# Token tiles turned by VectorE, a column-grouped gate, and seven early expert tiles in a top-2 expert layer

## The chip, the cores and the metric

The kernel runs on one core of a Trainium2 chip. The metric is device time in microseconds, the median of the runs shown. The core's engines run their own instruction streams and meet at semaphores: PE (TensorE) multiplies, DVE (VectorE) and ACT (ScalarE) work on its results, POOL (GpSimd) issues the indirect DMAs, and SP (SyncE) issues plain ones. All float32 products of the expert layer are made of three float32r products (high by high, high part by low weight, low part by high weight).

## The reference

```python
W = weights[condition]                       # (64 sequences, 64, 64)
y = jnp.einsum('bct,bcd->bdt', x, W)         # x is (64, 64, 1024): 4096 tokens of 1024
logits = y @ W_gate + b_gate                 # 8 experts
_, top_idx = jax.lax.top_k(logits, 2)
y_all = jax.nn.relu(jnp.einsum('bsd,edh->bseh', y, W_e) + b_e)
out = x + jnp.take_along_axis(y_all, top_idx[..., None], axis=2).mean(axis=2)
```

Each token goes through two of eight 1024x1024 experts, chosen by its own logits.

## The kernel before, in words

**Token tiles.** The 4096 tokens are 32 tiles of 128 rows, in eight groups of G = 4. For each tile `product` multiplies the block-diagonal condition matrices by the tile of x (two matmuls, 512 columns each) into `psO`; ACT copies it to `ys`, with the features of one token put in four quarters, and sends it to `y_rows` in DRAM, from which tokens are later gathered. PE turns `ys` with eight transposes into `psT` (`transposes`), ACT copies it out as the high part (`high`), DVE takes the low part (`low`). When a group is turned, `gate` multiplies it by the gate's weights in 16 matmuls of 512 columns; `unstack` turns the logits back; DVE picks the two experts of each token (`logits`, `choose`, `masks`); `ranks` counts on PE which slot each choice takes in its expert's list; `slots` makes addresses; POOL's `route` writes the token numbers to `slot_table` in DRAM, eight indirect DMAs a group.

**Expert tiles.** A tile is 128 slots of one expert, 48 matmuls of 512 columns (`products`). The first EARLY = 5 belong to expert 0 and are gathered straight from `y_rows` by a few indices (`early`), turned by PE and multiplied before the whole table is known. The rest wait for it: ACT reads all of `slot_table`, DVE makes the indices, POOL gathers each tile with four indirect DMAs (`gather`), DVE turns it with one 32x32-block transpose (`turn_rows`), ACT and DVE make the high and low parts (`parts`), PE multiplies (`all_products`), DVE adds the bias (`finish`), ACT takes the relu and half, and POOL adds the rows to `out` with an accumulating scatter. `schedule` on DVE works out which tile belongs to which expert; its result is needed by the first tile past the early ones.

**What sets the order.** Every stream is written by hand and in order; a wait holds up all that stands behind it on its engine. On SP, `turn` loads the tile of x four ahead when a product is done. `out` must first hold x, because the results are added to it: twelve tiles are stored from SBUF (`store`, slots 2 and 3 of the middle groups), and ten copies of two tiles each go from DRAM to DRAM (`copy`) behind the last load. Expert 0's weights are loaded in eight chunks by POOL and split into high and low parts on ACT and DVE (`split_first`), expert 1's by SP behind the copies. Per group PE runs four products, four sets of transposes, two halves of a gate, an `unstack` and a `ranks`.

## Time and profile before

| what | us |
|---|---|
| median of three runs | 924.06 (922.05 to 924.29) |
| profiled execution, its own time | 923.56 |
| its span in the trace | 921.8 |

The span runs from the first to the last record; 1.8 us of the time lie around it. A timeline row gives start, duration, engine, line and what it writes and reads, with the idle time ahead of it and who ended that. "PEclk" is the clock that TensorE was granted, as a share of 2.4 GHz.

### The profile page before, as it was taken

What the parts mean: (1) busy time and instruction counts of PE and PEld (TensorE: products, weight loads), DVE (VectorE), ACT (ScalarE), POOL (GpSimd) and SP (SyncE); (2) the same over time, 40 slices, a digit from 0 to 9 for tenths busy, and PEclk for the clock granted to TensorE, in tenths of its full rate; (3) what the DMA queues carried; (4) which work ended last, traced back from release to release, by engine and by line L of the source; (5) the groups of instructions that cost most, each with busy time, mean ns of one, the idle gap of its engine ahead of it and who ended that gap; (6) DMA issues with size and microseconds to landing.
All of it is one profiled execution on the core that took longest, in us unless ns stands there. A gap on an engine that the chain in (4) does not pass through costs nothing.

```text
span 921.8 us, 16408 instructions
## 1 busy us (share of the span) xinstructions
PE 892.2 (97%) x3988; PEld 702.6 (76%) x3989; DVE 408.6 (44%) x600; ACT 293.0 (32%) x383; POOL 497.7 (54%) x549
## 2 busy tenths in 40 slices
PE   8899989999999999999999999999999999999992
PEld 5455547788888888888888888888888888888882
DVE  4376776246373337333733354335533543333320
ACT  6586852225152123111521141113321421112210
POOL 4036465457666655655565546753655475555420
PEclk9999998999999999999999999999999999999997
DMA  8999979939686449454864476545854645444433
GB/s 320 402 368 361 374 290 319 304 82 256 158 284 133 102 94 292 95 111 97 260 138 97 91 201 186 110 103 127 254 110 92 193 102 114 91 97 98 81 46 46
DMA packets 51391, 163.11 MB, mean 177 GB/s; under 512 B 14178, under 2 KB 14178, under 8 KB 51202
## 3 DMA queue, kind: packets, MB, share of 16 engines
q0 software_dynamic: 26480, 77.78, 39.1%
q1 hardware_dynamic: 18546, 67.65, 20.5%
q10 hardware_dynamic: 6336, 17.34, 4.8%
q8 instruction: 12, 0.20, 0.1%
q14 instruction: 17, 0.14, 0.0%
HBM read 102.28 MB, written 70.94 MB: 188 GB/s over the span
## 4 chain that ended last, share of the span: by engine, by line
PE 87%; DMA 4%; POOL 3%; issue 3%; DVE 1%; SPq 0%; ACT 0%; ACTq 0%; POOLq 0%; DVEq 0%
PE psO L524 78%; PE psO L460 4%; DMA rows<-in_x 3%; POOL slot_table L344 3%; PE psT L476 2%; PE psG L486 1%; PE psG L488 1%; DMA rows<-y_rows,first 1%; PE psR L499 1%; POOL rows L359 0%; DVE w_lo L793 0%; POOL out L397 0%; SPq L271 0%; DVE rows L910 0%; DVE w_lo L797 0%
## 5 line engine op out<-in xcount | busy, mean ns | idle before, releaser
L524 PE MATMUL psO<-w_hi,a_hi 128*128 (+1 forms) x1104 | 340.6, 390 | 0.3 <-issue 0.3
L524 PE MATMUL psO<-w_lo,a_hi 128*128 (+1 forms) x1104 | 339.9, 389 | 0.0
L524 PE MATMUL psO<-w_hi,a_lo 128*128 (+1 forms) x1104 | 339.9, 389 | 0.0
L371 POOL DMA_INDIRECT rows<-y_rows,idx_g x256 | 263.8, 1030 | 110.6 <-issue 55.3
L524 PEld LDWEIGHTS psO<-w_hi,a_lo 128*128 128x128 f32 x1104 | 207.2, 188 | 43.1
L524 PEld LDWEIGHTS psO<-w_lo,a_hi 128*128 128x128 f32 x1104 | 207.2, 188 | 43.1
L524 PEld LDWEIGHTS psO<-w_hi,a_hi 128*128 128x128 f32 x1104 | 206.6, 188 | 43.5 <-issue 1.1
L935 DVE TENSOR_TENSOR a_lo<-ys,a_hi 128x1024 fp32r<-128x1024 f32 x64 | 78.4, 1226 | 115.3 <-ACT a_hi L693 115.3
L687 ACT ACTIVATE ys<-ys 128x1024 f32<-128x1024 f32 x34 | 36.1, 1061 | 271.3 <-DVE ys L910 271.3
L687 ACT ACTIVATE rows<-rows 128x1024 f32<-128x1024 f32 x35 | 37.1, 1061 | 265.8 <-DVE rows L910 265.8
L344 POOL DMA_INDIRECT slot_table<-toks,idx_all x64 | 64.1, 1002 | 77.1 <-DVEq L847 59.7
L910 DVE TENSOR_TENSOR ys<-psO,bias 128x1024 f32<-128x1024 f32 x34 | 41.6, 1222 | 135.1 <-PE psO L524 119.4
L910 DVE TENSOR_TENSOR rows<-psO,bias 128x1024 f32<-128x1024 f32 x35 | 42.8, 1224 | 129.0 <-PE psO L524 108.5
L924 DVE STREAM_TRANSPOSE ys<-rows 128x1024 f32<-128x1024 f32 x64 | 79.2, 1238 | 5.4 <-DMA rows<-y_rows,idx_g 5.2
L804 DVE TENSOR_TENSOR w_lo<-raw,w_hi 128x1024 f32 x56 | 65.1, 1222 | 34.4 <-ACT w_hi L641 34.4
L397 POOL DMA_INDIRECT out<-rows,idx_s x32 | 59.7, 1865 | 38.2 <-POOL idx_s L393 16.5
L397 POOL DMA_INDIRECT out<-ys,idx_s x32 | 55.5, 1736 | 42.0 <-ACT ys L687 20.7
L367 POOL COPY idx_g<-idx_all 128x4 uint32 x64 | 25.6, 400 | 88.1 <-issue 56.4
L693 ACT CAST a_hi<-ys 128x1024 fp32r<-128x1024 f32 x64 | 66.8, 1044 | 9.3 <-issue 8.9
L460 PE MATMUL psO<-rows,raw 128*128 128x512 f32 x128 | 62.3, 609 | 4.6 <-DMA rows<-in_x 4.0
L793 DVE TENSOR_TENSOR w_lo<-psT,w_hi 128x512 fp32r<-128x512 f32 x64 | 41.4, 686 | 40.4 <-ACT w_hi L627 37.4
L641 ACT CAST w_hi<-raw 128x1024 f32 x56 | 55.1, 1048 | 3.0 <-DMA raw<-in_L_ffn_W_e 2.2
(115 smaller groups left out, 417.0 us busy)
## 6 DMA issues: line engine op xcount, KB each, us to landing
raw<-in_L_ffn_W_e SPq DMA_DIRECT2D x56, 512.0 KB, 6.0
rows<-in_x SPq DMA_DIRECT2D x32, 512.0 KB, 7.2
y_rows<-ys ACTq DMA_DIRECT2D x32, 512.0 KB, 7.3
out<-rows SPq DMA_DIRECT2D x12, 512.0 KB, 6.3
bias<-in_L_ffn_b_e SPq DMA_DIRECT2D x8, 512.0 KB, 7.6
rows<-y_rows,idx_g POOLq DMA_INDIRECT x256
raw<-in_L_ffn_W_e POOLq DMA_DIRECT2D x4, 512.0 KB, 12.2
bias<-in_L_ffn_W_e POOLq DMA_DIRECT2D x4, 512.0 KB, 15.0
```

What stands on the lines that cost most here:

```text
L344: pool.indirect_dma_start(out=table, out_offset=bass.IndirectOffsetOnAxis(ap=adr[:, g, r, s:s + 1], axis=0), in_=toks[:, n:n + 1], in_offs ...
L371: pool.indirect_dma_start(out=rows[:, slot, a * DQ:(a + 1) * DQ], out_offset=None, in_=y_parts, in_offset=bass.IndirectOffsetOnAxis(ap=idx ...
L397: pool.indirect_dma_start(out=out, out_offset=bass.IndirectOffsetOnAxis(ap=idx_s[:, m:m + 1], axis=0), in_=o_sb[m], in_offset=None, comput ...
L460: last = nc.tensor.matmul(psO[s % 2][:, h * BANK:(h + 1) * BANK], bd[:, s, :], rows[:, s, h * BANK:(h + 1) * BANK], start=True, stop=True)
L524: last = nc.tensor.matmul(psO[p][:, h * BANK:(h + 1) * BANK], a[:, p, k * P:(k + 1) * P], w[:, bass.ds(slot + (k * H + h * BANK), BANK)], ...
L641: nc.scalar.copy(w_hi[:, bass.ds(at, H)], raw[:, k, :]).then_inc(s_hi, 1)
L687: nc.scalar.activation(o_sb[m], o_sb[m], ACTF.Relu, scale=0.5).then_inc(s_out, 1)
L693: nc.scalar.copy(a_hi[:, m % 2, :], ys[:, m % 2, :]).then_inc(s_ahi, 1)
L804: V.tensor_tensor(w_lo[:, bass.ds(at, H)], raw[:, k, :], w_hi[:, bass.ds(at, H)], ALU.subtract).then_inc(s_split, 1)
L910: V.tensor_tensor(o_sb[m], psO[m % 2][:, :], bias[:, bass.ds((e % 2) * H, H)], ALU.add).then_inc(s_bo, 1)
L924: V.transpose(ys[:, p, :].rearrange("p (k a i) -> p k a i", k=KD, a=Q), rows[:, p, :].rearrange("p (a k j) -> p k a j", k=KD, a=Q)).then_i ...
L935: V.tensor_tensor(a_lo[:, p, :], ys[:, p, :], a_hi[:, p, :], ALU.subtract).then_inc(s_alo, 1)
```

## The change

**Turning.** The eight PE transposes of each token tile, and of each early tile, are gone. DVE turns a token tile in one instruction, in 32x32 blocks, from `ys` to `turned` (`turn_tokens`); there is no split into high and low parts for the gate.

**Gate.** It is now 32 float32 matmuls a group: each takes one of 32 blocks of `turned` (128 columns) with 32 columns of a block-diagonal gate weight `wgb`, and writes to one of four 32-column groups of the array, in turn. One matmul against `stack` and one that adds the bias bring the logits back; `ranks` has seven small matmuls.

**Order.** The token loop is flat over n = 0..31. SP stores tiles 20 to 31 one at a time, each just ahead of the load that overwrites its buffer, and issues the ten copies, one a tile, with tiles 17 to 26. From group 0 on the slots of early tile t are read back when group t is routed (`read_first` on SP, `read_from` on DVE), and POOL fetches early tile t with four indirect DMAs ahead of the routing of group t + 2. Seven tiles are early; the first three are multiplied in quarters behind the products of token tiles 20 to 31, in a PSUM buffer of their own (`psE`). The other four follow the last token tile, with the last group's gate, `unstack` and `ranks` inside the first two. The slot table's layout is plain, and ACT reads it behind the high part of the last early tile.

```diff
-    STORED = 2
-    EARLY = 5
-    FLOOR = {NG - 5: EARLY - 2, NG - 4: EARLY - 1, NG - 3: EARLY}
+    EARLY = 7
+    MIXED = 3
...
+        STORES = range(5 * G, NTILE)
+        left = range(0, 5 * G, 2)
+        SPLITS = {2 * k + G + 1: k for k in range(KD)}
+        READS = {G * t + 3 * G: t for t in range(EARLY)}
+        FROM = {G * t + 3 * G + 2: t for t in range(EARLY)}
+        TURNS = {NTILE - 1 - G * MIXED + G * t: t for t in range(MIXED)}
+        TURNS[NTILE - 3] = MIXED
...
+                def read_first(t):
+                    sp.wait_ge(s_sc[t], LAND)
+                    for q in range(Q):
+                        sp.dma_start(read_at[q * R:q * R + Q, t, :].bitcast(U32), slots_of[t, :, :]
+                                     ).then_inc(s_first[t], 16)
+                    sp.dma_start(first[:, t:t + 1].bitcast(U32), slots_by[t, :, :],
...
+                for n in range(NTILE):
+                    if n in READS:
+                        read_first(READS[n])
+                    if n in STORES:
+                        store(n)
+                    if n < NTILE - G:
+                        sp.wait_ge(s_y, n + 1)
+                        if n in STORES:
+                            sp.wait_ge(s_xout[n % G], (n - STORES[0]) // G * 16 + 16)
+                        load(n + G)
+                    if n == STORES[0]:
+                        sp.wait_ge(s_split, KD)
+                        load_bias(0)
+                    c = n - (STORES[0] - 3)
+                    if 0 <= c < len(left):
+                        copy(c)
...
+                for g in range(2, NG):
+                    early(g - 2)
+                    route(g)
+                early(EARLY - 1)
...
+                    for b in range(NB):
+                        j = b % Q
+                        last = nc.tensor.matmul(psG[j * R:(j + 1) * R, 0:P], wgb[:, b, :], turned[:, g % 2, b, :],
+                                                start=(b < Q), stop=(b >= NB - Q), skip_group_check=True,
+                                                tile_position=(0, j * R))
...
+                for n in range(NTILE):
+                    g = (n - G) // G
+                    product(n)
...
+                    if g >= 0 and n % G == 1:
+                        gate(g)
+                    if g >= 0 and n % G == 2:
+                        unstack(g)
+                    if g >= 0 and n % G == 3:
+                        ranks(g)
+                    k = n - (NTILE - G * MIXED)
+                    if k >= 0:
+                        early_products(k // G, range(k % G * 2, k % G * 2 + 2))
+                early_products(MIXED, hooks={2: lambda: gate(NG - 1), 4: lambda: unstack(NG - 1)})
+                early_products(MIXED + 1, hooks={1: lambda: ranks(NG - 1)})
...
+                    V.transpose(turned[:, g % 2, :, s * R:(s + 1) * R],
+                                ys[:, s, :].rearrange("p (b i) -> p b i", i=R)).then_inc(s_turn, 1)
...
+                finish_early(MIXED - 1)
+                read_from(EARLY - 2)
+                choose(NG - 1)
+                turn_early(MIXED + 1)
+                early_lo(MIXED + 1)
+                slots(NG - 1)
...
+                finish_early(MIXED)
                 schedule()
...
+                turn_early(MIXED + 2)
+                early_lo(MIXED + 2)
+                read_from(EARLY - 1)
+                finish_early(MIXED + 1)
...
+                turn_early(MIXED + 3)
+                early_lo(MIXED + 3)
```

SP before, the end of the token loop (group 6's stores and the loads of group 7; `s_xout` is a store's landing, `s_y` a product's end):

```order
L243 DMA out<-rows 128x1024 [waits s_xin2]
L238 DMA rows<-in_x 128x1024 [waits s_y]
L243 DMA out<-rows 128x1024 [waits s_xin3]
L238 DMA rows<-in_x 128x1024 [waits s_y]
L238 DMA rows<-in_x 128x1024 [waits s_xout2,s_y]
L238 DMA rows<-in_x 128x1024 [waits s_xout3,s_y]
```

SP now, tiles 21 to 23 (`out<-in_x` is a DRAM-to-DRAM copy):

```order
L270 DMA out<-rows 128x1024 [waits s_xin1]
L266 DMA rows<-in_x 128x1024 [waits s_xout1,s_y]
L293 DMA out<-in_x 16x16384 [waits s_copy0]
L270 DMA out<-rows 128x1024 [waits s_xin2]
L266 DMA rows<-in_x 128x1024 [waits s_xout2,s_y]
L293 DMA out<-in_x 16x16384 [waits s_copy1]
L270 DMA out<-rows 128x1024 [waits s_xin3]
L266 DMA rows<-in_x 128x1024 [waits s_xout3,s_y]
L293 DMA out<-in_x 16x16384 [waits s_copy0]
```

Behind every store there now stands, as the next instruction, a load that waits for that store to land, and between a load and the next store there is a copy of 1 MB; before, a store had two loads between it and the one that waits for it, and the copies came behind all loads.

PE before, one token tile with the front of a gate (L460 is `product`, L476 a transpose, L486 and L488 the gate):

```order
L460 MATMUL psO<-rows,raw 128x512 [waits s_yc,s_bd,s_xin2]
L460 MATMUL psO<-rows,raw 128x512
L476 MATMUL psT<-ident,ys 128x128 [waits s_tc,s_yc]
L476 MATMUL psT<-ident,ys 128x128 x3
L476 MATMUL psT<-ident,ys 128x128 [waits s_tc]
L476 MATMUL psT<-ident,ys 128x128 x3
L486 MATMUL psG<-w_hi,a_hi 16x512 [waits s_tc,s_LT]
L488 MATMUL psG<-w_lo,a_hi 8x512
```

PE now, token tile 28 (L491) and the first quarter of early tile 2 (L541):

```order
L491 MATMUL psO<-rows,raw 128x512 [waits s_yc,s_bd,s_xin0]
L491 MATMUL psO<-rows,raw 128x512
L541 MATMUL psE<-w_hi,a_hi 128x512 [waits s_bo,s_split,s_alo]
L541 MATMUL psE<-w_hi,a_hi 128x512
L541 MATMUL psE<-w_lo,a_hi 128x512 x2
L541 MATMUL psE<-w_hi,a_lo 128x512 x2
L541 MATMUL psE<-w_hi,a_hi 128x512 x2
L541 MATMUL psE<-w_lo,a_hi 128x512 x2
```

The transposes are gone from between the products, and the quarter of an early tile takes their place; its first matmul waits for the bias addition of the early tile before it (`s_bo`), since both use `psE`.

ACT before, at the read of the whole slot table (L719; L652 and L627 bring in and split the early tiles 3 and 4):

```order
L687 ACTIVATE rows<-rows 128x1024 [waits s_bo]
L627 CAST a_hi<-psT 128x512 [waits s_t,s_mm]
L627 CAST a_hi<-psT 128x512 [waits s_t]
L719 DMA idx_all<-slot_table 32x1024 [waits s_sc5,s_sc4,s_sc6,s_sc3,s_sc7,s_sc2,s_sched,s_sc1,s_sc0]
L719 DMA idx_all<-slot_table 32x1024 x3
L652 COPY ys<-rows 128x1024 [waits s_t,s_yx0]
```

ACT now, at the same read (L701; L659 is the high part of an early tile, here of 4, 5 and 6):

```order
L659 CAST a_hi<-bias 128x1024 [waits s_mm,s_zt]
L653 ACTIVATE ys<-ys 128x1024 [waits s_bo]
L659 CAST a_hi<-bias 128x1024 [waits s_mm,s_zt]
L653 ACTIVATE rows<-rows 128x1024 [waits s_bo]
L659 CAST a_hi<-bias 128x1024 [waits s_mm,s_zt]
L701 DMA ys<-slot_table 32x8x128 [waits s_sc5,s_sc6,s_sc4,s_sc7,s_sc3,s_yout0,s_sc2,s_turn,s_sc1,s_sc0]
L701 DMA ys<-slot_table 32x8x128 x3
L653 ACTIVATE rows<-rows 128x1024 [waits s_bo]
```

The read stood ahead of the last early tile's steps (`unfold(4)` and `high`) and now stands behind the high part of the last early tile.

## Rows read from the trace of the kernel before

**Rows 1.** The page, part 1: busy us (share), instructions of each engine.
```profile
PE 892.2 (97%) x3988; PEld 702.6 (76%) x3989; DVE 408.6 (44%) x600; ACT 293.0 (32%) x383; POOL 497.7 (54%) x549
```

**Rows 2.** Timeline, PE, a token group: start us, us, engine, line, op [idle <-releaser].
```profile
107.90 1.88 PE L460 MATMUL psO<-rows,raw 128*128 128x512 f32 x4
109.72 1.16 PE L476 MATMUL psT<-ident,ys 128*128 128x128 f32 x8
110.64 0.48 PE L486 MATMUL psG<-w_hi,a_hi 128*16 128x512 f32 x1
...
123.72 1.88 PE L460 MATMUL psO<-rows,raw 128*128 128x512 f32 x4
```

**Rows 3.** Timeline, PE: product of tile 31; expert tile 5; last matmul.
```profile
128.62 1.96 PE L460 MATMUL psO<-rows,raw 128*128 128x512 f32 x4
...
207.85 0.62 PE L524 MATMUL psO<-w_hi,a_hi 128*128 x2
...
904.51 0.61 PE L524 MATMUL psO<-w_hi,a_lo 128*128 x2
```

**Rows 4.** Timeline, POOL: the last two slot scatters, and the last output scatter.
```profile
168.96 0.97 POOL L344 DMA_INDIRECT slot_table<-toks,idx_all  x1 [0.30 <-issue]
170.23 0.97 POOL L344 DMA_INDIRECT slot_table<-toks,idx_all  x1 [0.30 <-issue]
...
908.54 1.57 POOL L397 DMA_INDIRECT out<-rows,idx_s  x1 [3.73 <-ACT rows L687]
```

**Rows 5.** Groups by line and form: shapes, count, busy us, mean ns, idle before.
```profile
L924 DVE STREAM_TRANSPOSE ys<-rows 128x1024 f32<-128x1024 f32 x64 | 79.2, 1238 | 5.4 <-DMA rows<-y_rows,idx_g 5.2
...
L663 ACT COPY ys<-psO 128x1024 f32<-128x1024 f32 x32 | 32.4, 1012 | 26.4 <-PE psO L460 26.0
...
L815 DVE TENSOR_TENSOR idx_all<-idx_all,top 128x32 f32<-128x32 f32 x16 | 3.1, 197 | 0.6
```

**Rows 6.** DMA issues: count, KB each, median us to landing.
```profile
slot_table<-toks,idx_all POOLq DMA_INDIRECT x64, 6.8
...
idx_all<-slot_table ACTq DMA_DIRECT2D x4, 128.0 KB, 6.2
...
out<-in_x SPq DMA_DIRECT2D x10, 8.6
...
first<-slot_table ACTq DMA_DIRECT2D x8, 0.1 KB, 7.4
```

**Rows 7.** Line L243, the twelve stores out<-rows.
```profile
DMA to landing us min/median/max: 3.7/6.3/10.1
```

**Rows 8.** Line L238, the loads rows<-in_x.
```profile
DMA to landing us min/median/max: 4.8/7.2/12.1
```

**Rows 9.** Windows: us, busy and instructions of each engine, PEclk, DMA share, GB/s.
```profile
12.00:16.00 4.00, 4.00 (x22) 2.60 (x21) 1.87 (x5) 3.43 (x7) 1.08 (x2) 1.00 1.03 422
140.00:144.00 4.00, 4.00 (x14) 2.12 (x14) 3.02 (x14) 1.05 (x2) 3.09 (x4) 0.51 1.08 344
144.00:148.00 4.00, 4.00 (x24) 2.45 (x23) 2.33 (x15) 1.62 (x3) 0.15 (x1) 1.00 1.01 263
148.00:152.00 4.00, 4.00 (x21) 3.16 (x21) 3.07 (x12) 0.08 (x1) 2.92 (x3) 1.00 1.11 395
```

**Rows 10.** Timeline, PE, a wait and the transposes behind it.
```profile
137.54 1.94 PE L476 MATMUL psT<-ident,ys 128*128 128x128 f32 x8 [0.96 <-DVE a_lo L793]
```

**Rows 11.** Timeline, DVE: schedule's first instruction, and finish behind its last.
```profile
157.05 0.15 DVE L875 TENSOR_SCALAR cnt_f<-psR 1x8 f32<-1x8 f32 x1
...
163.03 1.23 DVE L910 TENSOR_TENSOR rows<-psO,bias 128x1024 f32<-128x1024 f32 x1 [0.22 <-DVE tile_s L898]
```

**Rows 12.** Timeline, DVE: slot indices ready; first gathered tile transposed and split.
```profile
189.99 0.75 DVE L968 TENSOR_SCALAR idx_all<-idx_all,part_q 128x1024 uint32<-128x1024 uint32 x1
...
200.40 1.25 DVE L924 STREAM_TRANSPOSE ys<-rows 128x1024 f32<-128x1024 f32 x1 [5.23 <-DMA rows<-y_rows,idx_g]
...
204.92 1.31 DVE L935 TENSOR_TENSOR a_lo<-ys,a_hi 128x1024 fp32r<-128x1024 f32 x1 [2.16 <-ACT a_hi L693]
```

More of the change, by code:

```diff
@@ L509, in ranks @@
-                    if g in FLOOR or g == NG - 1:
-                        last = nc.tensor.matmul(psR[:, total_at], ones, seen[:, G, :], start=True, stop=True)
-                    last.then_inc(s_rank, 1)
-                def products(t, e, slot, hooks={}):
+                    for a in range(Q - 1):
+                        nc.tensor.matmul(psR[:, (a + 1) * E:Q * E].rearrange("p (a e) -> p a e", e=E), ones,
+                                         mask[:, a:a + 1, :].to_broadcast([P, Q - 1 - a, E]), start=False, stop=False,
+                                         skip_group_check=True)
@@ L514, in products @@
+                def products(t, ps, e, slot, ks=range(KD), hooks={}):
                     n, half, m = t
                     p = m % 2
-                    for k in range(KD):
+                    for k in ks:
                         if k in hooks:
@@ L567, in _ @@
                     nc.tensor.matmul(psO[0][:, 0:P], ones, before, start=True, stop=True)
-                product(0)
-                product(1)
-                transposes(0)
-                pe.wait_ge(s_gw2, 1)
-                for g in range(NG):
-                    turn(g)
-                gate(NG - 1, 0)
-                gate(NG - 1, 1)
-                ranks(NG - 2)
-                transposes(NTILE + 1)
-                early_products(0, {1: lambda: unstack(NG - 1), 5: lambda: ranks(NG - 1)})
@@ L933, in parts @@
                     p = m % 2
[L934 removed]
+                    dve.wait_ge(s_ahi, n + 1)
                     V.tensor_tensor(a_lo[:, p, :], ys[:, p, :], a_hi[:, p, :], ALU.subtract).then_inc(s_alo, 1)
[L937 to L944 removed]
@@ L945, in _ @@
-                to_out(first_to[:, 0:EARLY - 2], first[:, 0:EARLY - 2], behind[:, 0:EARLY - 2])
-                dve.sem_inc(s_to, 1)
-                logits(NG - 1)
-                choose(NG - 1, 0)
-                choose(NG - 1, 1)
-                masks()
-                slots(NG - 1)
-                schedule()
-                finish_early(0)
-                low(NTILE + 2)
-                finish_early(1)
-                low(NTILE + 3)
-                for c in range(3, EARLY):
-                    dve.wait_ge(s_first[c - 2], 16 * Q)
@@ L960, in _ @@
-                to_out(first_to[:, EARLY - 2:EARLY], first[:, EARLY - 2:EARLY], behind[:, EARLY - 2:EARLY])
+                for n in range(NTILE):
+                    g = n // G - 1
+                    k = n - (NTILE - G * MIXED)
+                    if k >= 0 and k % G == 0:
+                        early_lo(k // G)
+                    if n == NTILE - 2:
+                        early_lo(MIXED)
+                    if g >= 0 and n % G == 2:
+                        choose(g)
+                    turn_tokens(n)
+                    if n == 2:
+                        gate_blocks()
+                    if g >= 0 and n % G == 3:
+                        slots(g)
+                    if n in SPLITS:
+                        split_first(SPLITS[n])
+                    if n in FROM:
+                        read_from(FROM[n])
+                    if n in TURNS:
+                        turn_early(TURNS[n])
+                    if k > 0 and k % G == 0:
+                        finish_early(k // G - 1)
```

720 lines of the change are left out of this document (320 added, 400 removed).

## Prediction

> **What bounds the kernel now.** The page's first part is read first: PE is busy for 892.2 us of the 921.8 us span [rows 1], so the question of every stretch is what keeps PE from its next matmul. The PE timeline then splits the span in three.
>
> In the token loop a group of four tiles takes 123.72 - 107.90 = 15.8 us, without a gap [rows 2]. A product takes 109.72 - 107.90 = 1.8 us and the eight transposes behind it 0.9. So 4 x 1.8 = 7.3 us a group are products, 4 x 0.9 = 3.7 are transposes and 4.8 are gate, `unstack` and `ranks`. The product of tile 31 ends near 130.4 [rows 3]; call this moment P.
>
> From expert tile 5 to the last matmul PE never waits: (905.1 - 207.85) / 64 = 10.9 us a tile, 69 tiles in all [rows 3]. Behind the last matmul come bias, relu, a scatter and its landing: 921.8 - 905.1 = 16.7 us, with POOL's last issue at 908.54 [rows 4]. I call T the moment when tile 7 starts: now 207.85 + 2 x 10.9 = 229.6. Nothing behind T is touched, and the tile count stays: worked out from the reference's inputs, expert 0 has 146, 268, 390, 528, 658, 778 and 913 rows after groups 0 to 6, so each of seven early tiles is full when its group is routed. Hence span = T + 62 x 10.9 + 16.7 = T + 692.2, and the change is worth what it does to T: to P, and to the way from P to T, now 99.2 us.
>
> **PE's own work.** The change takes 3.7 us of transposes and the old gate out of each group. The new gate is 32 matmuls of two records each, as a float32 product's two matmuls are four records in 1.8 us. A record of 128 columns is then 1.8 / 4 / 4 = 0.11 us, and 64 of them one after another take 7.3 us; if the four column groups run side by side, 1.8. No row shows column groups. I take 3.5, four at once and as much again for 64 loads of weights, and keep 1.8 and 7.3. With 0.5 for `unstack` and 0.5 for `ranks` (small matmuls, put at a tenth of a us each) a group is 7.3 + 3.5 + 1.0 = 11.8 us, and a pass without any wait would end 8 x 4.0 = 32 us sooner; the three mixed early tiles put 33 us of later work into the loop. If PE stayed the bound, T would be some 35 us earlier. It doesn't stay the bound, in three places.
>
> TensorEngine Tiling (Array Packing) in the Trainium skill, section Theoretical Speedup, promises up to 4x where the stationary side has 32 columns or fewer. By it the gate would be 1.8 us and the time 2 to 3 us lower than forecast; no run here shows it yet.
>
> **Place 1: routing paces tiles 0 to 20.** With the stores gone from the early groups, PE, DVE and the loads would allow some 3.4 us a tile. A group on PE is now 1.8 (product) + 3.5 (gate) + 1.8 + 0.5 (`unstack`) + a wait for `choose` + 0.5 + 1.8; `choose` has 14 instructions of 0.2 us and what lies between them [rows 5], 3.3 us, of which one product hides 1.8. On DVE it is four block transposes of 1.24 [rows 5], `choose`, `slots` and two splits, 11.6 us. POOL issues an indirect DMA each 170.23 - 168.96 = 1.27 us [rows 4]: 8 for a route and now 4 for an early tile, so 15.3 us a group. Step by step: the first nine products are bound by loads at 422 GB/s [rows 9] and end at 35; group 0's addresses come at 36, its scatters are issued by 46 and land at 52 (6.8 us behind the last issue [rows 6]). SP reads the slots back (five issues, 2 us, landing 7.4 [rows 6]): 61.5. Only then does POOL fetch early tile 0 (to 66.6) and route group 2 (to 76.9, landed 82.4). At tile 20 SP waits for just this, reads back (84.4), and issues the first store at 85. PE has been ready since 78.
>
> **Place 2: the stores hold up the loads of tiles 24 to 31.** Now each store is followed on SP by the load that waits for it, and ahead of the store stand, on the same queue, the load before it and a 1 MB copy. A load of 0.5 MB is 1.25 us at 422 GB/s. A copy moves at 263 GB/s where it is alone [rows 9], 4.0 us. So from one load to the next: 1.25 (load) + 4.0 (copy) + 1.25 (store) + some 2.2 for starting and landing (a lone store lands in 3.7, 2.4 more than its movement [rows 7]) = 8.7 us. The rows leave 7.2 (copy at 395 GB/s, [rows 9]) to 10 (the tile's y, 1.25, in its way too; twelve stores landed in 3.7 to 10.1 [rows 7]). Before, a store had two tiles of time to land. The first load goes at 85 + 4.5 = 89.5; then bias 1.3, a read-back 2.0, and seven steps of 8.7: the load of tile 31 goes at 153.7, lands 4.8 later [rows 8], and its product ends at P = 160.3. The early quarters fit in: a group on PE with an early tile is 11.8 + 10.9 + 3.7 (the wait for `psE`: ACT's copy 1.0, DVE's transpose 1.24, bias addition 1.2) = 26.4 us against 4 x 8.7 = 35.
>
> DMA: Bandwidth & Descriptors in the Trainium skill, section Queues, rings and completion order, says that on each DMA engine the descriptors of a queue are consumed in ring order. That speaks against this change, as it puts the store behind the copy; no row of before shows a store behind a copy. Were the store not held by it, a step would be 4.7 us, and PE's 26.4 us a group would bound this stretch instead; that is the first rival.
>
> **Place 3: from P to T.** Counted from P: `ranks` and the last quarter of early tile 2 to 3.2, DVE's bias addition to 4.9, two eighths of tile 3 to 7.7, the last gate to 11.2, two eighths to 13.9, `unstack` to 14.4, `choose` to 17.9. DVE then turns and splits early tile 4 (to 21.6; PE waits 1.8) ahead of `slots`; tile 4's first eighth and `ranks` end at 23.6, the addresses come at 24.5, POOL's eight issues end at 34.8. Meanwhile DVE does `schedule`, 163.0 - 157.05 = 5.8 us [rows 11], before it turns early tile 5, so that this is ready at 35.7 while PE is free at 33.1. Early tile 6 is fetched behind the last route (36.3 to 41.4), is turned at 44.8 and cast by ACT at 45.9. Only then ACT reads the table: four issues (1.7) and 5 us of landing ([rows 6]: 6.2), 52.5. Two DVE instructions make the indices, 55. From there the rows of before give the way: 200.40 - 190.74 = 9.7 us to the gathered tile and 206.2 - 200.4, less the work of 1.2 between, to its low part [rows 12]: 68.4. PE's four tiles end at 58.2, so it stands for 10 us, and its clock will fall. Before, behind waits of 1.9 and 0.96 us, the clock was 0.51 of full speed, its lower level of 1.2 GHz, for a whole window of 4 us [rows 9], and eight transposes took 1.94 us in place of 1.04 [rows 10]; that is 3 us for the start of tile 7, 2 for the smaller waits behind P and 1 for DVE, late with the read-back of early tile 4. From P to T: 68.4 + 6 = 74.5 (68 to 80).
>
> **The sum.** T = 160.3 + 74.5 = 234.8, 5.2 later than now. Span 234.8 + 692.2 = 927.0; with the 1.8 us around it 928.8, against 923.6 for the profiled execution of before, which is the median to 0.5. I say 929. With steps of 7.2 and 68 from P to T it would be 912, with 10 and 80, 943.
>
> **Rivals.**
> First, and on the other side: the stores don't queue behind the copies. From the moment when PE takes up early tile 0 (82.6) its own work sets P: 12 tiles at 26.4 / 4 and the tail of the group, P = 150. PE is busy, its clock stays, and P to T is 68. T = 218, time 912. For it speaks that a window with a copy under way moved 395 GB/s beside one with 263 [rows 9]: the engines had room. It decides once a step is under 6.6 us.
> Second: the column groups don't run at once. 7.3 us a gate make a group 15.6 us, as before, and 30.2 with an early tile. Group 2's addresses and the store of tile 20 come 12 us later, P = 172, and the gate behind P adds 3.8: T = 251, time 945. For it: each of the 32 matmuls takes all 128 rows, and no row shows an overlap.
> Third: the change doesn't do what it says. The read-backs queue behind loads and copies, early tile 0 comes after product 20, and in order on PE all later products wait for it; 10 us on P, time 939.
>
> **How the numbers follow.** The forecast has 0.50, spread over 918 to 938; the first rival 0.30, the second 0.15, the third 0.05. The range of 905 to 948 takes in the first and second rivals and leaves out a first rival with still shorter waits and a second with a slower clock. A measurement here can tell 0.3%, 2.8 us: 921.3 to 926.8 is no change. Of the forecast 0.15 lies there and 0.02 below it, of the first rival 0.02 there. Faster 0.30, same 0.17, slower 0.53.
>
> **What the profile of the changed kernel would show.** The gate's 64 records in 3.5 us or in 7.3. SP's first store near 85, and from there loads of x 8.7 us apart, each behind a store that landed; the windows there at a DMA share near 1 and PE waiting for x ahead of tiles 24 to 31. The last product's end near 160. Behind it waits of PE for the low parts of early tiles 4 and 5 and some 10 us ahead of tile 7, with a low clock, and ACT's read of the table behind the cast of early tile 6. From T on the same 10.9 us a tile. The prediction is wrong if the loads come 6 us apart or less, if POOL's routes come sooner so that tile 20 is stored well ahead of 80, or if P to T is under 65.

## The result and the profile after

The changed kernel takes 1083.68 us at the median of four runs (1078.13 to 1089.68), beside 924.17 us for the kernel before on the same chip (922.05 to 925.17): a ratio of 1.173, 95% interval 1.165 to 1.181. I had said 929, in a range up to 948. The sign was right, the size was wrong by 155 us.

The page of the changed kernel, its first part, then in slices of 1/40 of the span PE, the clock, the DMA engines' busy share and what they moved:

```profile
span 1086.0 us, 16371 instructions
PE 893.2 (82%) x4088; PEld 693.8 (64%) x4089; DVE 408.3 (38%) x515; ACT 256.6 (24%) x309; POOL 511.4 (47%) x560
...
PE   6850771272759588999999999999999999999994
...
PEclk9965786585788888999999999999999999999997
DMA  9999999884753779656754755484567455545432
GB/s 338 296 136 105 197 174 168 109 288 117 270 21 16 179 194 271 173 126 144 234 107 93 219 142 109 89 256 107 108 167 184 101 121 159 112 92 102 92 59 39
```

From slice 17 on it reads like the kernel before. Everything is lost ahead of that, and the last two rows have to be read together: in slices 3 to 8 the DMA engines are busy for 80 to 100% of the time and move 105 to 197 GB/s. Before, windows with a share of 1.01 to 1.11 moved 263 to 422 [rows 9]. The same in windows (busy time of each engine, granted clock, DMA share, GB/s):

```profile
20.00:50.00 30.00, 23.58 (x185) 12.14 (x186) 20.22 (x49) 18.08 (x33) 8.03 (x7) 0.93 1.05 353
50.00:80.00 30.00, 16.17 (x84) 7.33 (x82) 6.19 (x9) 5.04 (x9) 11.60 (x14) 0.61 1.09 134
80.00:110.00 30.00, 1.75 (x10) 1.24 (x10) 6.84 (x24) 3.20 (x7) 1.48 (x2) 0.56 0.94 114
110.00:140.00 30.00, 23.20 (x124) 12.14 (x127) 15.71 (x30) 10.79 (x19) 21.34 (x22) 0.76 1.17 185
```

The engines go from 353 to 134 GB/s without becoming less busy. The chain of waits says what happened at that moment (start, length, what the chain stood on):

```profile
40.15 1.67 POOL slot_table L380
...
49.24 0.97 POOL slot_table L380
50.20 0.31 issue
50.51 25.62 DMA slot_table<-toks,idx_all
77.47 29.37 DMA first<-slot_table
...
122.58 29.94 DMA slot_table<-toks,idx_all
...
154.25 28.23 DMA out<-rows
...
184.01 19.87 DMA out<-rows
```

POOL issues group 0's eight scatters of token numbers from 40.15 to 50. They land at 76.1, the read-back of `first` at 106.84. After the next route on the chain, group 2's, the landing takes 29.9 us, and the store and the load behind it wait in the same way. For all the kernel, from issue to landing (count, KB each, median us):

```profile
rows<-in_x SPq DMA_DIRECT2D x32, 512.0 KB, 10.1
y_rows<-ys ACTq DMA_DIRECT2D x32, 512.0 KB, 12.8
...
bias<-in_L_ffn_W_e POOLq DMA_DIRECT2D x4, 512.0 KB, 29.3
slot_table<-toks,idx_all POOLq DMA_INDIRECT x64, 14.1
```

The slot scatters had a median of 6.8 [rows 6] and the loads of x 7.2 [rows 8]; now 14.1 and 10.1. PE sees it as a wait for x (total, times, longest):

```profile
PE psO L491 <- DMA rows<-in_x: 113.0, 12, 24.9
PE psO L541 <- DVE a_lo L899: 19.9, 2, 11.5
PE psO L541 <- DVE a_lo L916: 13.2, 4, 4.9
```

**The error, piece by piece.** These are the marks of my sum. The product of tile 31, tile 7's first products and the end, on PE:

```profile
290.11 3.78 PE L491 MATMUL psO<-rows,raw 128*128 128x512 f32 x4 [5.82 <-DMA rows<-in_x]
...
380.37 1.22 PE L541 MATMUL psO<-w_hi,a_hi 128*128 x2 [4.91 <-DVE a_lo L916]
...
413.70 1.22 PE L541 MATMUL psO<-w_hi,a_hi 128*128 x2 [4.65 <-DVE a_lo L916]
```

| | forecast | changed kernel | off by |
|---|---|---|---|
| P, end of product 31 | 160.3 | 293.9 | 133.6 |
| P to T, start of tile 7 | 74.5 | 86.5 | 12.0 |
| T to the end of the span | 692.2 | 705.6 | 13.4 |
| span | 927.0 | 1086.0 | 159.0 |

The last of the three lines above the table is tile 9: tiles 7 and 8 take 33.3 us in place of 21.8, most of the third row of the table. The experiments are about these rows, the first above all.

### The profile page after: what moved, and what is told of

It reads as the page before. It is cut to its first block, busy times and chain, and to the rows that moved or that the text cites. A ratio compares the mean times of both kernels' runs of the same rounds, so it can differ in the third digit from the quotient of the medians.

```text
span 1086.0 us, 16371 instructions
## 1 busy us (share of the span) xinstructions
PE 893.2 (82%) x4088; PEld 693.8 (64%) x4089; DVE 408.3 (38%) x515; ACT 256.6 (24%) x309; POOL 511.4 (47%) x560
## 4 chain that ended last, share of the span: by engine, by line
PE 61%; DMA 23%; DVE 4%; POOL 3%; issue 3%; another core or an unknown queue 2%; SPq 1%; ACT 1%; ACTq 1%; DVEq 0%; POOLq 0%
PE psO L541 59%; DMA out<-rows 10%; DMA slot_table<-toks,idx_all 5%; DMA first<-slot_table 3%; PE psO L491 1%; POOL slot_table L380 1%; DMA raw<-y_rows,from_q 1%; POOL rows L408 1%; DMA rows<-in_x 1%; DMA raw<-in_L_ffn_W_e 1%; DMA wgc<-wgc 1%; POOL raw L394 1%; DMA rows<-y_rows,idx_g 0%; PE psE L541 0%
## 5 line engine op out<-in xcount | busy, mean ns | idle before, releaser
L541 PE MATMUL psO<-w_hi,a_hi 128*128 (+1 forms) x1040 | 326.2, 395 | 33.2 <-DVE a_lo L899 19.9
L541 PE MATMUL psO<-w_lo,a_hi 128*128 (+1 forms) x1040 | 324.1, 393 | 0.0
L541 PE MATMUL psO<-w_hi,a_lo 128*128 (+1 forms) x1040 | 323.6, 393 | 0.0
L541 PEld LDWEIGHTS psO<-w_hi,a_hi 128*128 128x128 f32 x1040 | 197.5, 191 | 77.3 <-DVE a_lo L899 21.2
L541 PEld LDWEIGHTS psO<-w_lo,a_hi 128*128 128x128 f32 x1040 | 198.1, 190 | 41.7
L541 PEld LDWEIGHTS psO<-w_hi,a_lo 128*128 128x128 f32 x1040 | 197.5, 190 | 41.7
L491 PE MATMUL psO<-rows,raw 128*128 128x512 f32 x128 | 86.4, 818 | 118.6 <-DMA rows<-in_x 113.0
L491 PEld LDWEIGHTS psO<-rows,raw 128*128 128x128 f32 x128 | 29.2, 247 | 153.6 <-DMA rows<-in_x 121.0
L394 POOL DMA_INDIRECT raw<-y_rows,from_q x28 | 27.4, 978 | 175.6 <-DVEq L866 166.6
L778 DVE STREAM_TRANSPOSE turned<-ys 128x1024 f32<-128x1024 f32 x32 | 39.4, 1239 | 100.5 <-ACT ys L629 98.1
## 6 DMA issues: line engine op xcount, KB each, us to landing
rows<-in_x SPq DMA_DIRECT2D x32, 512.0 KB, 10.1
```

The source lines that it names most:

```text
L394: pool.indirect_dma_start(out=fetched[t % 2][:, a * DQ:(a + 1) * DQ], out_offset=None, in_=y_parts[0:(P + (t + 1) * G * P) * Q, :], in_off ...
L491: last = nc.tensor.matmul(psO[n % 2][:, h * BANK:(h + 1) * BANK], bd[:, s, :], rows[:, s, h * BANK:(h + 1) * BANK], start=True, stop=True)
L541: last = nc.tensor.matmul(ps[:, h * BANK:(h + 1) * BANK], a[:, p, k * P:(k + 1) * P], w[:, bass.ds(slot + (k * H + h * BANK), BANK)], star ...
L778: V.transpose(turned[:, g % 2, :, s * R:(s + 1) * R], ys[:, s, :].rearrange("p (b i) -> p b i", i=R)).then_inc(s_turn, 1)
```

## Experiments

Chips differ: in four of the comparisons the kernel before took 924.2 to 927.4 us, in the fifth, on a chip of its own, 947.1. Where two kernels didn't run on the same chip I compare ratios to the kernel before on the chip of each. That is good to some 1.6% where the 947.1 us chip is one of the two: one and the same kernel, the last of this section, has a ratio of 1.028 there and 1.012 on another chip. A run of an experiment without an interval is a single execution; executions of one kernel on one chip lay up to 1.4% apart.

**Theories.** A: the new layout of the slot table. Before, rank r of an expert went to word (r mod 32) x 1024 + column, so that consecutive ranks lay 4 KB apart; now it goes to expert x 4096 + r, and the 128 words of a scatter fall in runs of some sixteen neighbours. B: the read of `first`, 128 single words for each early tile, now in SP's queue. C: my own second place, the order of stores, copies and loads.

### Which part of the change it is

Two kernels write the slots to a second region which nobody reads; the region that is read keeps its spare rows. All waits, sizes and counts stay. One takes the old addresses, one the new.

```
+ own(V.tensor_copy(pi, place))                     # e1_spread
+ V.tensor_scalar(hi, pi, 5, None, logical_shift_right)
+ own(V.tensor_scalar(lo, pi, 31, None, bitwise_and))
+ own(V.tensor_scalar(hi, hi, 32768, None, add))
+ own(V.scalar_tensor_tensor(adr, lo, 1024, hi, mult, add))
- own(V.tensor_copy(adr, place))
+ own(V.tensor_scalar(adr, place, 32768, None, add)) # e1_adj
```

> Edit: the slot scatters of the changed kernel write to a second half of the table, which nobody reads, at the addresses of the kernel before (consecutive ranks 4 KB apart); the half that is read keeps its spare rows, so every gather fetches rows of zeros and the expert results go to rows that are thrown away. The number and size of the writes, their queue and all waits are those of the changed kernel. Theory A (words written next to one another hold the 16 DMA engines up): the median landing of a slot scatter falls from 14.1 us to about 7, the loads of x no longer need 15 to 30 us in 50 to 280 us, and the time falls from 1084 to 915 to 950 us. Theory B (the reads of single words of the table into first are what clogs): nothing changes, 1060 to 1100 us. Theory C (the order of stores, copies and loads in SP's queue): nothing changes either, 1060 to 1100 us.

> Control for the run with spread addresses: the same second half of the table and the same rows of zeros, but the words stay at the changed kernel's addresses (consecutive ranks next to one another). Theories A, B and C all expect the changed kernel's time, 1060 to 1100 us, with landings of the slot scatters of about 14 us at the median; a time well under that would say that the gathers of real rows, not the addresses, are the cost.

Measured: 954.8 us spread, 1038.8 adjacent, the kernel before 927.3. The same 64 scatters of the same 128 words cost 84 us more by their addresses alone. The windows from 50 to 110 us, first spread, then adjacent:

```profile
50.00:80.00 30.00, 25.20 (x186) 12.68 (x184) 23.32 (x61) 16.61 (x30) 24.07 (x24) 0.87 1.01 373
80.00:110.00 30.00, 23.33 (x139) 16.35 (x139) 14.51 (x40) 7.21 (x14) 15.31 (x16) 0.79 0.88 329
```

```profile
50.00:80.00 30.00, 15.59 (x91) 7.00 (x89) 9.97 (x24) 7.90 (x15) 11.38 (x13) 0.67 1.07 156
80.00:110.00 30.00, 16.05 (x96) 7.37 (x96) 13.66 (x34) 8.70 (x16) 14.27 (x14) 0.67 0.96 220
```

At the same share the engines move 373 GB/s or 156. The adjacent control is 45 us faster than the changed kernel itself, which it should have equalled by all theories. It doesn't read back the lines that are being written, and it fetches rows of zeros; which of the two matters was not tried. With spread addresses the same two differences cost nothing (1.030 here, 1.027 in the kernel below that reads its table back), so the rows of zeros alone don't explain it.

The other way round, the kernel before with adjacent addresses and nothing else of the change:

```
- own(V.scalar_tensor_tensor(adr, rank_row, Q * COLS, col, mult, add))
+ own(V.scalar_tensor_tensor(adr, col, R, rank_row, mult, add))   # col moved into the second region
```

> Edit: the kernel before with its slot scatters at plain addresses (consecutive ranks next to one another), into a second half of the table that nobody reads; expert results go to rows that are thrown away. Nothing else of the change is in it. Theory A: the landing of a scatter rises from 6.8 us at the median to 12 or more, each route is followed by 20 to 40 us of slow loads, and the kernel takes 970 to 1080 us. Theories B and C: 924 us within 1%, since neither its read-backs nor its stores are touched.

Measured: 1020.9 us against 927.3. Median landing of a slot scatter 15.2 us, of a load of x 10.9, and the window 50 to 80:

```profile
50.00:80.00 30.00, 23.54 (x114) 13.39 (x112) 14.79 (x48) 16.24 (x30) 17.36 (x18) 0.91 1.07 201
```

One line of the address arithmetic, put into the old kernel, costs 94 us. That is theory A from the other side. Theory B:

```
- sp.dma_start(first[:, t:t + 1], slots_by[t, :, :], allow_slow_non_contiguous=True)
+ own(V.tensor_copy(first, short_i.to_broadcast([P, EARLY])))    # once, ahead of all
```

> Edit: the changed kernel without the seven reads of 128 single words into first (its values are set by VectorE, so the results of the seven early tiles go to rows that are thrown away); the reads in four rows of 32 words stay. Theory B: the stretches of slow loads shrink and the time falls to 920 to 980 us. Theory A: the time falls by 0 to 30 us at most (the one read of 29.4 us on the chain of waits goes, the clogging does not), 1050 to 1084 us. Theory C: as A.

Measured: 1078.8 us, 4.8 below the changed kernel's median and inside that kernel's own spread. The 29.37 us on the chain were a victim: with that read gone, the window 80 to 110 still moves little:

```profile
80.00:110.00 30.00, 4.27 (x13) 1.99 (x12) 8.54 (x24) 3.86 (x7) 4.52 (x5) 0.50 1.01 132
```

Theory B is out as the cause of the whole.

### What in the layout it is

Consecutive ranks at a distance of W words, in the unread region:

```
- own(V.tensor_copy(adr, place))
+ own(V.tensor_scalar(adr, place, W, 32768, mult, add))
```

> Edit: the changed kernel with its slot scatters into a region that nobody reads, in the order of the ranks but with neighbouring ranks 64 bytes apart instead of 4 (as in the control, the gathers fetch rows of zeros and the expert results are thrown away). The two controls measured 1038.8 us (4 bytes apart) and 954.8 us (4 KB apart). Theory A1 (writes of single words are slow when several of them fall into one line of 64 bytes): about 955 us, 945 to 975. Theory A2 (what counts is that writes in flight go to one small stretch of DRAM, some hundred bytes to kilobytes): 1000 to 1045 us.

> Edit: as the run with 64 bytes between neighbouring ranks, with 512 bytes. Theory A1: about 955 us, the same as with 64 bytes. Theory A2: between that run and 955 us; if 64 bytes measures over 1000, 512 bytes measures 955 to 990.

> Edit: as the run with 64 bytes between neighbouring ranks (952.1 us), with 32 bytes; 4 bytes measured 1038.8. The scatters go to a region that nobody reads, the expert results are thrown away. Theory A1 with a line of 64 bytes: two words of a scatter now share a line instead of sixteen, so a small part of the 87 us comes back, 955 to 975 us. Theory A1 with a line of 32 bytes or less: 952 us as with 64 bytes, within 3.

> Edit: as above with 16 bytes between neighbouring ranks. A line of 64 bytes: four words share it, 965 to 1000 us. A line of 32 bytes: two words share it, 955 to 975. A line of 16 bytes or less: 952 us.

> Edit: as the run with 16 bytes between neighbouring ranks, with 8 bytes: eight words of a scatter share a line, a route and an expert fill 1 KB. Theory H with a cost for every word beyond the first in a line: 1.05 to 1.09, between 16 bytes (1.037) and 4 bytes (1.12). A threshold would give 1.03 to 1.04 or 1.11 to 1.13. Theory I (a stretch of 512 bytes): 1.03 to 1.05.

| distance of consecutive ranks | words in 64 bytes (in 16) | us | before, same chip | ratio | PE's waits for x | median landing of a slot scatter |
|---|---|---|---|---|---|---|
| 4 bytes | 16 (4) | 1038.8 | 927.3 | 1.120 | 76.2 | 12.3 |
| 8 bytes | 8 (2) | 1005.1 | 925.1 | 1.086 | 51.8 | 9.5 |
| 16 bytes | 4 (1) | 981.6 | 947.1 | 1.036 | 6.9 | not recorded |
| 32 bytes | 2 (1) | 982.6 | 947.1 | 1.037 | 5.9 | not recorded |
| 64 bytes | 1 (1) | 952.1 | 927.4 | 1.027 | 13.4 | 5.3 |
| 512 bytes | 1 (1) | 952.4 | 927.4 | 1.027 | 10.4 | 5.6 |
| 4 KB | 1 (1) | 954.8 | 927.3 | 1.030 | 10.4 | 4.6 |

From 64 bytes on distance is worth nothing. The 1% that 16 and 32 bytes stand above that lies within the 1.6% by which their chip raises a ratio, so it is no cost. PE's waits for x say it more plainly, first at 8 bytes and then at 16 (on the chip of the latter the last kernel of this section waits 4.6 us, on another chip 8.9):

```profile
PE psO L492 <- DMA rows<-in_x: 51.8, 11, 9.9
```

```profile
PE psO L492 <- DMA rows<-in_x: 6.9, 4, 3.3
```

So the cost sets in between 16 and 8 bytes and grows from 8 to 4. Theory A1 with a line of 64 bytes and a cost for every further word expected 16 bytes to stand well above 32; they are equal. The unit in which words meet may be 64 bytes with a cost only above four words, or 32 or 16 bytes; these runs don't tell. Where the texts below say "a line of 64 bytes", that size is an assumption.

Two runs put the words of a line and the size of the stretch against each other. In the first, ranks are permuted inside a tile's 128 words; the readers need no change, since where a token stands in its tile does not matter:

```
- own(V.tensor_copy(adr, place))
+ adr = (place & ~127) + (place & 7) * 16 + ((place >> 3) & 15)      # six small operations
```

> Edit: the changed kernel with the word of rank r put at place (r mod 8) x 16 + (r / 8) of its 128 words, by six small VectorE operations in each group; where a token stands within its tile of 128 does not matter, so all readers stay as they are. Consecutive ranks are 64 bytes apart, and eight ranks later the next word falls into the line of the first, so a scatter has about two words in a line instead of sixteen. Theory A1 (words in a line): 950 to 985 us. Theory A2 (a small stretch of DRAM, here still 512 bytes for each tile): above 1030 us.

Measured: 1058.3 us, ratio 1.117, median landing 30.2. PE waits 79.1 us for x. This kernel reads its table back, so it stands beside the changed kernel (1.173, 113.0 us) and not beside the control: the permutation takes about a third of the cost away. Two thirds stay, where I had expected 950 to 985 us. I had counted the words that one scatter puts into a line, two. Two things can be behind that. A route has eight scatters under way at once, and an expert's 128 words of a route still fill the same eight lines, sixteen words to each. Or the two words of one scatter are enough: ranks r and r + 8 stand 4 bytes apart. No run separates these. A third possibility was that only the stretch of 512 bytes matters. In the second run lines of sixteen ranks stay whole, and each lies 4 KB from the next:

```
+ adr = 32768 + (place >> 4) * 1024 + (place & 15)
```

> Edit: the changed kernel with its slot scatters into a region that nobody reads, sixteen consecutive ranks in one line of 64 bytes as in the changed kernel, but each line 4 KB from the next (the expert results are thrown away). Ratios to the kernel before on the same chip so far: words 4 bytes apart 1.12, 16 or 32 bytes 1.037, 64 bytes 1.027, within a tile's 512 bytes 64 bytes apart 1.117. Theory H (sixteen words written into one line of 64 bytes within one route, by one scatter or by its eight, are what is slow): 1.09 to 1.14. Theory I (the words of a route and an expert all fall into a stretch of 512 bytes, whatever the line): 1.02 to 1.04, since each stretch now holds sixteen words.

Measured: 1031.2 us, ratio 1.115, median landing 13.3, PE's waits for x 75.8 us: the cost of the adjacent control (1.120, 12.3, 76.2). So no stretch longer than 64 bytes is needed: words packed 4 bytes apart into pieces of 64 bytes are slow wherever the pieces are. And all other traffic is slow with them.

DMA: Bandwidth & Descriptors in the Trainium skill, section Why small descriptors are slow (HBM only), gives small descriptors an overhead for each packet and for its metadata. That goes by size and number, which are the same in all these runs; by it they would all take the same time, and they lie 87 us apart. Here the address decides.

### The layout repaired, and then my second place

The changed kernel with the old layout and readers to fit (the whole computation is in it):

```
- slots_of, slots_in, slots_by by t, a, (i o)
+ slots_at = table.rearrange("(i c) o -> i (c o)", i=R)
+ slots_by = table.rearrange("(i c a) o -> i c (a o)", i=R, a=Q)
...
+ sp.dma_start(read_at[q * R:(q + 1) * R, t, :], slots_by[:, t, :])   # x4, of 32 x 16 bytes
- own(V.transpose(read_t, read_at[:, t, :]))
+ own(V.tensor_scalar(from_q[:, t, :], read_at[:, t, :], Q, part_q, mult, add))
+ adr = (place & 31) * 1024 + (place >> 5)
```

> Edit: the changed kernel with the table laid out as in the kernel before (row = rank modulo 32, 4 KB apart), and its two readers changed with it: each early tile reads its words in 4 transfers of 32 x 16 bytes and takes first from them on VectorE, the whole table comes back in 4 transfers of 32 rows of 4 KB. The rest of the change is kept. Theory A: the time falls from 1084 to 930 to 960 us; what is left above my forecast of 929 is then in the stores and in the seven early tiles. Theory C (the order of stores, copies and loads): above 1030 us.

Measured: 952.3 us (948.0 to 956.8), ratio 1.027, interval 1.021 to 1.034. The layout costs 131 us of 1083.7 (two chips, on which the kernel before took 924.2 and 927.4), and what is left is a kernel on which my sum can be tried step by step. Theory C, as the cause of the whole, is out. Product 31 and tile 7 on PE:

```profile
175.72 3.66 PE L489 MATMUL psO<-rows,raw 128*128 128x512 f32 x4 [2.73 <-DMA rows<-in_x]
...
245.54 1.22 PE L539 MATMUL psO<-w_hi,a_hi 128*128 x2 [5.07 <-DVE a_lo L918]
```

P is 179.4 and T 245.5. SP's queue shows my second place in the clear; a store, and then the load that waits for it:

```profile
90.02 0.47 SPq L270 DMA_DIRECT2D out<-rows  x1
97.27 0.35 SPq L266 DMA_DIRECT2D rows<-in_x  x1
...
98.72 0.58 SPq L270 DMA_DIRECT2D out<-rows  x1
108.41 0.34 SPq L266 DMA_DIRECT2D rows<-in_x  x1
...
163.89 0.62 SPq L270 DMA_DIRECT2D out<-rows  x1
172.25 0.33 SPq L266 DMA_DIRECT2D rows<-in_x  x1
```

The first store goes at 90.0 (forecast 85), the first load behind one at 97.3 (89.5), the last at 172.25 (153.7). The seven steps with the bias load and the read-back between them are 75.0 us, 10.7 each, where I had 64.2, 9.2 each. Without the 3.3 us that I put at those two it is 10.2 against 8.7. To see whether this order is what sets P, the stores and copies of the kernel before were put in: two tiles of each of groups 1 to 6 stored, two tiles ahead of the load that waits, and the ten copies behind the last load.

```
- STORES = range(5 * G, NTILE)
+ STORED = [n for n in range(G, NTILE - G) if n % G >= 2]
+ if n % G < 2 and n + 2 in STORED: store(n + 2)
- c = n - (STORES[0] - 3); copy(c)
+ if n >= NTILE - G: copy(n - (NTILE - G))      # the rest ahead of the last two read-backs
```

> Edit: as the run with the table of the kernel before, and also the stores and copies of the kernel before: two tiles of each of groups 1 to 6 are stored (issued two tiles ahead of the load that waits for them), and the ten copies come behind the last load instead of between the stores. Theory D (my forecast's second place: the chain of store, wait and load in SP's queue, some 10 us for each of twelve tiles, costs 20 to 30 us): 905 to 930 us, 15 to 40 under the run before this one. Theory E (the DMA engines carry the same bytes in either order and the last tokens come no sooner, or the gap after the last product is what costs): within 8 us of the run before this one.

Measured: 942.2 us (941.2 to 947.4), ratio 1.018, interval 1.013 to 1.024; 10 us under the run before it, on the same chip. P came from 179.4 to 168.2, so the gain is where theory D puts it, though it is below the 15 to 40 us that D expected, and above E's 8: the early quarters on PE pace these tiles next. A group with an early tile takes 27.9 us from product to product (138.43 to 166.32 for tiles 27 and 31), without a wait for x and with one of 5.1 us for `o_first`, the result of the early tile before; in all there are three of these, 12.3 us:

```profile
138.43 1.88 PE L490 MATMUL psO<-rows,raw 128*128 128x512 f32 x4
...
166.32 1.88 PE L490 MATMUL psO<-rows,raw 128*128 128x512 f32 x4
```

```profile
PE psO L540 <- DVE a_lo L919: 15.6, 3, 7.0
PE psE L540 <- DVE o_first L881: 12.3, 3, 5.1
```

### The third row of the sum: tiles 7 to 9

In all of these kernels tiles 7 to 9 don't follow each other in 10.9 us. In the one above, tile 7 starts at 235.39 and tile 9 at 269.46, 34.1 us for 21.8 of work. On POOL the scatters of the early tiles stand between the gathers, and each waits for the landing of the one before:

```profile
237.47 1.62 POOL L421 DMA_INDIRECT out<-o_first,first_to  x1 [0.30 <-issue]
244.15 1.56 POOL L421 DMA_INDIRECT out<-ys,first_to  x1 [5.06 <-DMA out<-o_first,first_to]
245.17 1.16 POOL L403 COPY idx_g<-idx_all 128x4 uint32 x1
```

The fourth scatter waits 5.06 us for the third to land, and the gather of tile 9 stands behind it. So the scatters were moved up by one place each:

```
+ scatter_early(0)
  early(EARLY - 1)
+ scatter_early(1)
  pool.wait_ge(s_idx, 1)
  gather(tile(0, EARLY))
+ scatter_early(2)
  gather(tile(0, EARLY + 1))
  scatter_early(3)
```

> Edit: the kernel with the table and the stores of before (942.2 us), with the scatters of the early tiles moved up by one place in POOL's order: the first ahead of the fetch of early tile 6, the second ahead of the wait for the table, the third behind the gather of tile 7, and so on. Theory F (tiles 8 and 9 wait in that kernel for 3.2 and 5.4 us because VectorE stands at the wait for the third early scatter, which lets it split the next weights over the first results, and because each scatter waits for the one before): 930 to 938 us. Theory G (the gathers themselves, 4 transfers and about 5 us each on POOL, pace these tiles): within 3 us of 942, and not under 939.

Measured: 974.3 us beside 947.1 for the kernel before, ratio 1.028. It fell on the slower chip and its partner had not: inconclusive. The pair was run again on one chip.

> The kernel with the table and the stores of the kernel before once more, to stand beside the next on one chip. It gave a ratio of 1.018 to the kernel before (1.013 to 1.024); all theories expect that again, 1.01 to 1.03.

> The kernel with the scatters of the early tiles one place up in POOL's order, on the same chip as the run without it. Theory F (tiles 8 and 9 wait for the third early scatter and for those behind it): 0.5 to 1.3% under that run, and the waits of tiles 7 to 9 on a_lo fall from 15.6 us to about 10. Theory G (the gathers pace these tiles): within 0.3% of it, the same waits in sum.

Measured: 941.5 us (938.3 to 942.7) without, 935.7 (934.4 to 937.4) with the move, 0.6% less and inside theory F's 0.5 to 1.3%, ratios 1.018 (1.015 to 1.022) and 1.012 (1.009 to 1.015). PE's waits for the gathered tiles, first without and then with it:

```profile
233.64 1.21 PE L540 MATMUL psO<-w_hi,a_hi 128*128 x2 [6.08 <-DVE a_lo L919]
249.72 0.72 PE L540 MATMUL psO<-w_hi,a_hi 128*128 x2 [2.88 <-DVE a_lo L919]
267.82 1.21 PE L540 MATMUL psO<-w_hi,a_hi 128*128 x2 [6.93 <-DVE a_lo L919]
```

```profile
236.88 1.22 PE L539 MATMUL psO<-w_hi,a_hi 128*128 x2 [5.48 <-DVE a_lo L918]
251.71 0.72 PE L539 MATMUL psO<-w_hi,a_hi 128*128 x2 [2.30 <-DVE a_lo L918]
264.35 0.73 PE L539 MATMUL psO<-w_hi,a_hi 128*128 x2 [1.47 <-DVE a_lo L918]
```

Tiles 7 to 9 take 27.5 us in place of 34.2; T itself comes 3.2 later: 1.3 of that is there at P already, and the rest may be the scatter that now stands ahead of a fetch. The gain is at tile 9, whose gather stood behind POOL's wait. The half of theory F that put the wait on VectorE's splitting of the weights did not show: tile 8 gained 1.3 us.

No version beat the kernel before. The best of them, with three repairs, is 1.2% above it.

## Why the prediction was wrong, and where it was right

**Place 1 fell, at one number.** "Its scatters are issued by 46 and land at 52 (6.8 us behind the last issue [rows 6])", and the same for group 2. (46 and 6.8 make 52.8; that slip is not what failed.) The 6.8 was measured with words 4 KB apart, and the change rewrites exactly the addresses. I counted the change's DMAs, their sizes and their queues, and took the landing over without asking what it depended on; the new row was 25.62 us, then 29.94. It also had no bound of its own, so the range could not hold it: with my bounds P went to 169, and in the second rival to 172. The cost reached past the scatters: every load, store and fetch beside them slowed down (353 GB/s to 134). Of the 133.6 us on P, the repaired layout takes 114.5 back (293.9 to 179.4).

**Place 2 was right in mechanism and short in size.** Once the layout was repaired, SP's chain of store, wait and load stood where I put it, and taking it away moved P by 11.2 us and the time by 10.1. Freed of bias and read-back the step is 10.2 us, not 8.7, just beyond the 10 that I had as its upper bound; the start is 7.8 later. 7.8 + 10.8 + 0.5 for the last landing are the 19.1 us between 179.4 and 160.3.

**Place 3: P to T** is 66.1 us in the kernel with the repaired layout and 67.2 with the old stores too, less than my 74.5 and just below my range of 68 to 80. The read of the table is where I put it: with the repaired layout ACT issues it 46.6 behind P (forecast 45.9), the indices are ready at 53.0 (55) and the low part of tile 7 at 65.7 (68.4; my own terms, 55 + 9.7 + 4.6, make 69.3). What was mis-sized is the 6 us that I added for a low clock: from P to T the granted clock is 0.92, 0.92, 0.99 and 0.94 (to 200, 220, 235 and 245.5 us). The low clock does come, but behind T: after PE's wait of 5.07 us (I had 10) it is 0.50, the lower level of 1.2 GHz, from 245.5 to 249.5. In the changed kernel P to T is 86.5: the waits for early tiles 4 and 6 (11.55 and 8.38 us) came with the slow traffic.

**"Nothing behind T is touched" was false.** Seven scatters in place of five stand in POOL's order between the gathers of tiles 7 to 11. From T to the end takes 704 to 707 us in all kernels with the new order, against 692.2, and 698.0 (934.9 - 236.9) with the scatters moved up. I had counted the tiles behind T but not the scatters that fall due there. Moving them up takes 7.6 of the 13.4 us back (705.6 to 698.0 on one chip). Of the other 5.8 the low clock at the start of tile 7 is a part; the rest stays open.

**The gate** took 1.95 to 2.7 us for its 64 records, not 3.5 and not 7.3. The last one in the changed kernel:

```profile
303.74 1.95 PE L502 MATMUL psG<-turned,wgb 128*32 128x128 f32 x64
```

The four column groups run at the same time, and the second rival (they don't) is out. TensorEngine Tiling (Array Packing) in the Trainium skill, section Theoretical Speedup, promised up to 4x; against the 7.3 us of my estimate the trace shows 3.7x. By that rule the trace agrees. It bought little here: also with the repaired layout and the old stores PE is not what this stretch waits for, as that kernel's window from 50 to 80 us shows.

```profile
50.00:80.00 30.00, 24.79 (x185) 12.48 (x184) 22.16 (x58) 16.32 (x29) 21.36 (x22) 0.83 1.03 399
```

PE works for 24.8 of 30 us, beside DMA engines that are full and move 399 GB/s.

**The rivals.** The first (stores don't queue, PE bound, 912) never showed in the order of the change; its PE bound of 26.4 us a group shows as 27.9 with the stores of the kernel before, and even then the time was 942. It was mis-summed too: 82.6 and 12 x 6.6, less the 3.2 us that stand behind product 31, give P near 158 and a time near 920, not 150 and 912. The third (read-backs late, PE held by early tile 0) has one thing in common with what happened: SP's loads stand behind a read-back that waits for its scatters to land. But PE waits 5.1 us for early tile 0 and 113.0 for x, and the delay on P is 133.6 us in place of 10.

In sum: of 155 us, 131 are the layout. The rest is on the span of the repaired kernel, 952.2 against 927.0: P 19.1 later, 8.4 less from P to T, 14.5 more behind T. That the sign came out as forecast is no merit of the sum: my forecast sat 5 us above the kernel before, and the layout, which decided it, was not in it.

**Left open.** Why the changed kernel is 45 us slower than its control with the same addresses and no read-back of the written lines. How wide the unit is in which words meet (16, 32 or 64 bytes), and whether the words of one scatter are enough or those of a route's eight count together. And where they meet, in the DMA engines or behind them in the memory; the records show only that the packets take longer.

## What to carry to other kernels

When a change rewrites addresses, the landing times of the old addresses are no longer a price; give the new pattern bounds of its own, also where only a few bytes are moved. Scattered single words into DRAM don't belong 4 or 8 bytes apart within what is under way at once; 64 bytes are enough, and at 16 no cost was seen here. A DMA share near 1 beside a fraction of the usual GB/s is the sign that they stand too close, and a control that moves only the addresses settles it. When a boundary is drawn behind which "nothing is touched", count what the change makes due behind it, queue by queue.

## What the runs showed of the hardware

- 64 scatters of 128 words of 4 bytes, 32 KB in all, cost 84 us of an otherwise equal kernel through their addresses alone (1038.8 against 954.8), and 94 us in the kernel before (1020.9 against 927.3).
- The cost goes by how close the words lie: consecutive words 4 bytes apart 1.120 of the time before and 76.2 us of PE's waits for x, 8 bytes 1.086 and 51.8, 16 and 32 bytes 1.036 and 1.037 (on the chip that raises ratios by 1.6%) and 6.9 and 5.9, 64 bytes to 4 KB 1.027 to 1.030 and 10.4 to 13.4. It doesn't go by the distance between packed pieces of 64 bytes (64 bytes apart 1.120, 4 KB apart 1.115), and permuting the words inside the same 512 bytes takes only about a third of it away (1.173 to 1.117, the latter on the slower chip).
- Transfers of other queues suffer with them: median landing of a 0.5 MB load of x from 7.3 to 10.6 us, at a DMA share of 1.07 and 156 GB/s in place of 1.01 and 373.
- Four column groups of 32 columns do run at the same time: 64 records of 128 columns in 1.95 us, where one after another, at the 0.11 us of a record in the kernel before, they would take 7 us (an estimate).
